# Four phases of a conditioned transformer in one program per engine, with the first sequences of a phase placed in the last iterations of the phase before it

## The reference

```python
# layer 0
h = film(rmsnorm(x, norm1_w), cond, film1_w, film1_b)        # x*(1+scale)+shift, per sequence
Q, K, V = h @ q_w + q_b, h @ k_w + k_b, h @ v_w + v_b
attn = softmax(einsum('bnd,bmd->bnm', Q, K) * D ** (-0.5))   # one head
x = x + (einsum('bnm,bmd->bnd', attn, V) @ proj_w + proj_b)
h = film(rmsnorm(x, norm2_w), cond, film2_w, film2_b)
x = x + gelu(h @ mlp_w1 + mlp_b1) @ mlp_w2 + mlp_b2          # 256 -> 1024 -> 256, erf gelu
# layer 1: cmod = silu(cond) @ w_ada + b_ada gives shift, scale and gate twice
k, q, v = split(modulate(layernorm(x), shift_msa, scale_msa) @ w_qkv)   # 16 heads of 16
w = softmax(einsum('bqhc,bkhc->bhqk', q / CH, k))
x = x + gate_msa * (einsum('bhqk,bkhc->bqhc', w, v) @ w_proj + b_proj)
h = gelu(modulate(layernorm(x), shift_mlp, scale_mlp) @ w_mlp1 + b_mlp1) # tanh gelu
x = x + gate_mlp * (h @ w_mlp2 + b_mlp2)
```

## Time and profile before

| | |
|---|---|
| median of 3 runs | 1713.98 us (1713.98 to 1715.13) |
| the profiled execution | 1714.05 us |
| its span in the profile | 1712.1 us |
| PE busy | 1623.0 us, 95% of the span |
| DVE, ACT, POOL busy | 1279.9, 867.3, 477.7 us |
| mean granted clock of PE | 0.98 of full speed |

### The profile page before, as it was taken

The page is one execution under the profiler, slowest core; times in us unless marked ns, Lnnn a source line. Parts: engine busy times, 40 slices in busy tenths (PEclk is TensorE's granted clock), DMA queues, the critical chain, the costliest instruction groups (busy, mean ns, idle before and its releaser), DMA issues. The chain is left out here.

```text
span 1712.1 us, 42938 instructions
## 1 busy us (share of the span) xinstructions
PE 1623.0 (95%) x14686; PEld 1455.3 (85%) x14686; DVE 1279.9 (75%) x2831; ACT 867.3 (51%) x1756; POOL 477.7 (28%) x633
## 2 busy tenths in 40 slices
PE   7999998999999997799999999999995999999998
PEld 6999997999999997577777777777763999999998
DVE  3798886676666664688888888888883777777776
ACT  1576663333333333577777777777764333333332
POOL 1333231122121212134333333433323121222211
PEclk8999999999999998899999999999997999999999
DMA  6500001000000000433333333333330111111111
GB/s 201 161 22 19 21 16 52 3 3 1 0 0 0 0 0 7 127 101 107 103 99 102 106 103 98 103 100 98 102 92 20 38 48 40 48 38 49 37 49 37
DMA packets 99465, 100.60 MB, mean 59 GB/s; under 512 B 13745, under 2 KB 89841, under 8 KB 99393
## 3 DMA queue, kind: packets, MB, share of 16 engines
q1 hardware_dynamic: 96784, 99.53, 18.5%
q10 hardware_dynamic: 2448, 0.08, 0.1%
q0 software_dynamic: 160, 0.04, 0.1%
HBM read 38.62 MB, written 8.55 MB: 28 GB/s over the span
## 5 line engine op out<-in xcount | busy, mean ns | idle before, releaser
L1403 DVE TENSOR_REDUCE C_negmax<-bank 128x4 f32<-128x1024 f32 x256 | 313.3, 1224 | 77.9 <-PE bank L1233 74.5
L1339 ACT ACTIVATE C_probs<-bank 128x1024 f32<-128x1024 f32 x256 | 262.1, 1024 | 116.6 <-PE bank L1247 113.8
L897 ACT ACTIVATE B_g<-bank,B_bias 128x256 f32<-128x256 f32 x256 | 107.3, 470 | 226.4 <-PE bank L198 208.6
L897 ACT ACTIVATE D_g<-bank,D_bias 128x256 f32<-128x256 f32 x256 | 107.3, 470 | 218.9 <-PE bank L198 218.9
L1233 PEld LDWEIGHTS bank<-C_kx,C_qs 64*128 64x128 f32 x1024 | 77.8, 187 | 114.6 <-DVE C_negmax L1403 78.4
L1233 PE MATMUL bank<-C_kx,C_qs 64*128 64x256 f32 x1024 | 130.5, 333 | 29.1 <-DVE C_negmax L1403 12.4
L198 PE MATMUL bank<-B_wt_w_hi,B_g_lo 128*128 128x256 f32 x512 | 147.6, 288 | 4.3 <-DVE B_g_lo L926 4.1
L198 PE MATMUL bank<-D_h_hi,D_wt_w_lo 128*128 128x256 f32 x512 | 147.6, 288 | 1.8 <-DVE D_h_lo L323 1.8
L198 PE MATMUL bank<-D_wt_w_hi,D_g_lo 128*128 128x256 f32 x512 | 146.9, 287 | 2.5 <-DVE D_g_lo L926 1.9
L198 PE MATMUL bank<-B_h_hi,B_wt_w_lo 128*128 128x256 f32 x512 | 147.2, 288 | 1.8 <-DVE B_h_lo L323 1.8
L198 PE MATMUL bank<-B_h_hi,B_wt_w_hi 128*128 128x256 f32 x512 | 145.5, 284 | 0.0
(11 more groups left out here) (263 smaller groups left out, 5090.0 us busy)
## 6 DMA issues: line engine op xcount, KB each, us to landing
C_qs<-C_q_hi SPq DMA_DIRECT2D x128, 128.0 KB
C_kx<-C_k_hi SPq DMA_DIRECT2D x128, 128.0 KB, 2.1
C_qs<-C_q_lo SPq DMA_DIRECT2D x64, 128.0 KB
C_kx<-C_k_lo SPq DMA_DIRECT2D x64, 128.0 KB, 2.1
C_gbc<-mod_rows SPq DMA_DIRECT2D x32, 256.0 KB, 3.4
D_gbc<-mod_rows SPq DMA_DIRECT2D x32, 256.0 KB, 3.3
out<-xres SPq DMA_DIRECT2D x32, 256.0 KB, 3.5
xres<-in_x SPq DMA_DIRECT2D x4, 1792.0 KB, 16.3
```

The costliest lines, as they stand in the source:

```text
L897: ins = eng.activation(g[u][:, d * S:(d + 1) * S], hbank[u][:, d * S:(d + 1) * S], func, bias=per_seq(bias1, 2 * u + d, b))
L1339: e_exp.by(eng.activation(probs[t % NP][:, :], stpair[:, :], ACT.Exp, scale=scl))
L1403: e_max.by(eng.tensor_reduce(m4[:, :, :, j], spair[:, :].rearrange("p (e q k) -> p e q k", e=2, q=TH), AX, ALU.max, negate=True))
```

## The change

One block holds the program of each engine for all four phases, one behind the other; the barriers between the phases are gone (the prologue keeps its block). Steps for the first sequences of a phase ("heads") are called from the last iterations of the phase in front:

- in A: stats, root, xhat, transposes and both splits of B's sequence 0. B then begins at iteration 1 (`START`).
- in B, iterations 28 to 32 (`TAIL` leaves four more iterations of B written out, so that they can differ): the first fill of C's stacks, stats, root, xhat, transposes and splits of C's sequences 0 and 1, q and k of sequence 0 with their splits, and on SP, behind the preparation's loads, the placing of q and k of sequence 0 (`head_place`, 14 transfers). C begins at iteration 1, without the tasks in `TAKEN`.
- in C: stats, root, xhat, transposes, splits of D's sequences 0 and 1, all four up products, gelus and splits of sequence 0 and three of its four down products; load and splits of D's `w2` in four parts; the first two loads of D's gates. D begins at iteration 2.

So that this can be, the norm has two sets of buffers (A and C, B and D), B and D use other banks, the tiles lie in other places, and where tiles of two phases share memory a wait stands in the program: `e_res.wait(..., LAST)`, the last residual of the phase in front, on ACT before B's first gelu, on POOL, on SP before the first loads, and at the start of C's ACT, POOL and SP programs. The once-only loads of C's and D's gate rows are made from `gates` directly. The core of the diff, without the lines that only change their indentation:

```diff
-def run_pipeline(eng, n_seq, max_skew, iteration):
+def run_pipeline(eng, n_seq, max_skew, iteration, first=0, tail=0):
-    for i in range(PEEL):
+    for i in range(first, PEEL):
         iteration(Seq(None, i))
-    with eng.Fori(PEEL // UNROLL, n_seq // UNROLL) as j:
+    with eng.Fori(PEEL // UNROLL, (n_seq - tail) // UNROLL) as j:
...
-    for i in range(n_seq, n_seq + max_skew):
+    for i in range(n_seq - tail, n_seq + max_skew):
...
+        attention_norm, mlp_norm = NormBuffers("a_"), NormBuffers("m_")
...
# phase A
+                NEXT_PE = {"B T": 541}
+                NEXT_ACT = {"B hi": 546}
+                NEXT_DVE = {"B stats": 523, "B xhat": 536.5, "B lo": 547}
+                NEXT_POOL = {"B root": 527}
...
# phases B and D
+                if l1:
+                    hbank, tbank = banks[:4], banks[4]
+                else:
+                    hbank, tbank = [banks[i] for i in (0, 1, 3, 4)], banks[2]
+                obank, head_bank = [banks[7], banks[5]], banks[7]
+                START, TAIL = (2, 0) if l1 else (1, 4)
...
                 def tensor(eng):
                     def it(i):
                         f, m, r = i, i.back(1), i.back(2)
+                        last = i.off if not l1 and i.reg is None else None
                         up(eng, m, 0)
                         down(eng, r, 3)
                         up(eng, m, 1)
                         down(eng, m, 0)
+                        if last == NB - 1:
+                            heads["C"].head_k(eng)
                         up(eng, m, 2)
                         down(eng, m, 1)
                         if f.exists(NB):
                             norm.e_lo.wait(eng, f.back(1))
                             norm.transpose(eng, f)
+                        if last in (NB - 2, NB):
+                            heads["C"].head_T(eng, last - NB >= 0)
                         up(eng, m, 3)
...
                         down(eng, m, 2)
+                        if last == NB - 2:
+                            heads["C"].head_q(eng)
...
                 def scalar(eng):
+                        if last == 1:
+                            prev.e_res.wait(eng, LAST)
+                        if last == NB - 1:
+                            heads["C"].head_hi(eng, "q")
                         for u in range(3):
                             gelu(eng, m, u)
+                        if last in (NB - 4, NB - 3):
+                            heads["C"].head_stacks(eng, last - NB + 4)
+                        if last == NB - 1:
+                            heads["C"].head_hi(eng, "k")
                         if f.exists(NB):
                             norm.evac_hi(eng, f)
+                        if last in (NB - 2, NB):
+                            heads["C"].head_hi(eng, "h", last - NB >= 0)
...
+                    def sync(eng):
+                        prev.e_res.wait(eng, LAST)
+                        prep.sync(eng)
+                        heads["C"].head_place(eng)
...
# phase C
+                NEXT_PE = {"D T": 525.95, "D up0": 538, "D up1": 540, "D T1": 541, "D up2": 547.6, "D up3": 548,
+                           "D down0": 549.5, "D down1": 550.5, "D down2": 555}
+                NEXT_ACT = {"D hi": 525.98, "D w2 hi0": 535.1, "D w2 hi1": 536.1, "D w2 hi2": 537.1, "D w2 hi3": 540,
+                            "D hi1": 540.3, "D gelu0": 542.1, "D gelu1": 542.2, "D gelu2": 544.6, "D gelu3": 546}
+                NEXT_DVE = {"D stats": 516, "D xhat": 521, "D lo": 535, "D stats1": 535.01, "D xhat1": 538.7, "D lo1": 543.99,
+                            "D split0": 552, "D split1": 553, "D split2": 560.1, "D split3": 560.2}
+                NEXT_POOL = {"D root": 517, "D w2 lo0": 543.4, "D w2 lo1": 543.5, "D root1": 535, "D w2 lo2": 543.8,
+                             "D w2 lo3": 543.9, "D xb": 560}
+                NEXT_SP = {"D w2": 532, "D gates": 553, "D gates1": 554}
+                TAKEN = [(n, 0) for n in ("lo_q", "lo_k", "z0", "z1", "q0", "q1", "k0", "k1")] + [
+                    (n, 1) for n in ("stats", "root", "xhat", "T", "hi_h", "lo_h")]
...
+                        if b.reg is None and (name, b.off) == ("q", 1):
+                            prev.e_res.wait(eng, Seq(None, NB - 2))
+                        if b.reg is None and (name, b.off) == ("M0", 0):
+                            prev.e_res.wait(eng, LAST)
+                    def d_T(b):
+                        e_vev.wait(eng, LAST)
+                        heads["D"].norm.transpose(eng, FIRST, heads["D"].head_bank)
+                    def d_up(b, u):
+                        (e_max if u < 2 else e_exp).wait(eng, LAST, NT)
+                        heads["D"].up(eng, FIRST, u)
...
+                    prev.e_res.wait(eng, LAST)
+                    eng.wait_ge(s_pad, 1)
+                    init_stacks(eng, 1)
...
+        with nc.Block() as blk:
+            @blk.tensor
+            def _(eng):
+                for n in "ABCD":
+                    heads[n].tensor(eng)
...
```

More of the change, by code:

```diff
@@ new lines, in down @@
+                def down(eng, b, u):
+                    if not b.exists(NB):
+                        return
+                    if l1 and b.reg is None and b.off == 0:
+                        eng.wait_ge(w2.s_lo, u + 1)
+                        if u == 0:
+                            norm.e_lo.wait(eng, SECOND)
+                    e_glo.wait(eng, b, u + 1)
+                    if u == 0:
+                        e_res.wait(eng, b.back(UNROLL))
+                    for h in range(TH):
+                        for d in range(2):
+                            c = slice(d * S + h * P, d * S + (h + 1) * P)
+                            ins = mm3(eng, obank[b.par][:, h * D:(h + 1) * D],
+                                      [((g_hi[u][:, c], g_lo[u][:, c]), w2.part(2 * u + d, 0, D))],
+                                      start=u == 0 and h == 0 and d == 0, stop=u == 3 and d == 1, skip=True)
+                    e_mm2.by(ins)
@@ new lines, in qk_cm @@
+                def qk_cm(eng, b, name, bank=None):
+                    bank = mbank(name) if bank is None else bank
+                    norm.e_lo.wait(eng, b)
+                    w_hi, w_lo = w_qk[name]
+                    for t in range(KT):
+                        c = [slice(k * D + t * P, k * D + (t + 1) * P) for k in range(KT)]
+                        ins = mm3(eng, bank[:, t * S:(t + 1) * S],
+                                  [((w_hi[:, c[k]], w_lo[:, c[k]]), norm.tokens(b, k)) for k in range(KT)])
+                    done[name].by(ins)
@@ new lines, in hi_bias @@
+                def hi_bias(eng, b, name, bank=None):
+                    bank = mbank(name) if bank is None else bank
+                    landed, dmas = (s_qd, Q_DMAS) if name == "q" else (s_kd, K_DMAS)
+                    prev_b = b.back(1)
+                    if not prev_b.before_first():
+                        for w in range(2):
+                            eng.wait_ge(landed[w][prev_b.par], (prev_b.pair + 1) * dmas * 16)
+                    done[name].wait(eng, b)
+                    for t in range(KT):
+                        c = slice(t * S, (t + 1) * S)
+                        ins = eng.activation(qk[name + "_hi"][:, c], bank[:, c], ACT.Identity, bias=per_seq(prep.bias[name], t, b))
+                    done_hi[name].by(ins)
```

1469 lines of the change are left out of this document (796 added, 673 removed).

## The result

The changed kernel takes 1672.82 us (median; executions from 1669.01 to 1675.84), the kernel before, run beside it, 1714.51 us: a ratio of 0.9756, 95% interval 0.973 to 0.9781. The forecast was 1670.0 in 1660 to 1686.

The account below looks back on a forecast made before the run. PE, busy 95% of the span, was taken to set the pace, with time to gain only where it idles or runs slowly. 7.5 + 17.5 + 19 = 44 us off 1714 gave 1670 us, range 1660 to 1686.

Parts of the forecast that it names:

- A to B: Change from phase A to B: first down product 7.5 us earlier, near 266.1; bounds 5 and 8.5 us.
- The rule of the added drain: Table switches at B's gelu and in D: the skill's drain would cost 1.4 us more each, 2.8 in all.
- B to C: Change from phase B to C: 17.5 us earlier, 16 of it at C's first score product; bounds 12 and 19.
- The 1.5 us for the clock: C's start: q product of sequence 1 at the upper clock gives back 12 x (0.245 - 0.119) = 1.5 us.
- C to D: Change from phase C to D: D's steady part 19 us earlier; bounds 14.7 and 23.5 us.
- hold the exponential chain by ...: C's tail: up groups and AV's product hold exponentials 2.9 us, w2 pieces 0.9, evacuation 0.2; last ends near 1301.9, not 1297.9.
- Within a steady iteration nothing changes: Steady loops: only bank numbers and buffer places change, costed at nothing, since PE at 99% and 97% covers them.
- The signs named: Profile after: B's first down product near 266, C's first score near 664.5, its eighth 15 to 17 us later.
- The drains only stretch: Rival, all three seams: drains lengthen, only barrier, norm and placing are saved, 24.6 us, giving 1689 us; chance 0.21.
- The barrier stays in another form: Rival, phase changes: waits for the last residual keep heads from running earlier, time within 0.2%, 1713 us; chance 0.02.
- The thin stretches stay cold: Rival, C's first two iterations and D's head: low clock costs 5 us, 1675 us; included in the 0.74 case.
- a head step stop PE for 3 us: Slower rival, last iterations: the change loses once 14 inserted PE steps wait 3.1 us each on average; chance 0.03.

Follow-up runs that it names:

- the first profile: Profiled execution of the changed kernel as it stands, beside the trace of the kernel before: 1675.45 us, span 1673.5 us.
- the second profile: The changed kernel, unaltered, profiled again beside the later experiments; its median there was 1671.92 us.

## Why the prediction was right, and where it was not

The total was met within 3 us, partly by luck: two seams gave 6 to 8 us less than forecast, and B's loop gave 5.7 that no step had.

*A to B: 7.5 taken, about 6 us at the higher clock and 4.6 in the first profile, below the bound of 5.* These are the ledger's 7.08 and 5.66 less the 1.1 us by which A's last three residuals lie further apart than before (17.83 us, 16.74 before); in two other traces with A unchanged they are 17.4 and 17.7 us apart, so with only the 0.4 of the wait taken off it is 6.7 and 5.3. The longer wait at A's end (0.4) and the table load (1.28, no more) came as walked. Residual to first down product shrank by 6.98, so 6.6 net: of the missing 0.9, half is the subtraction at 1.10 us beside POOL's addition, for which I took the 0.69 that a lone one needs, the rest ACT's start 0.5 us behind the residual. The difference of the two profiles is the clock. In the first profile it fell behind PE's wait of 2.48 us (0.68 granted in the 5 us behind it), in the second it did not behind 2.47 us (1.00), and the ledger's row differs by 1.4 us accordingly. The rule of the added drain, weighed in the prediction at 2.8 us for both switches, has no trace in any run: from the end of the exponential to the start of the gelu it is 1.32 us, load included.

*B to C: 17.5 taken, 17 measured.* The ledger gives 19.43 + 0.68 less 3.1 for the products that moved into B; undoing the head gives 17 to 18, of which 2.5 are that run's own. The walk held in its parts: the transposes, q and k fit B's iterations, the last iteration waits 0.71 us, the transfers went out on SP from 641.87 on, the second pair of fills costs DVE 0.27 us of waiting for q. The 1.5 us for the clock did not come as told: the q product of sequence 1 ran at the upper level, but the clock fell at 669.8, and the end of k and all of v ran at 0.21 us each. That is also the price of a matmul at the lower level: the prediction's 0.245 is a group's length through twelve, and the rows of before start 0.21 us apart, so twelve give back 1.1 us and not 1.5.

*C to D: 19 taken, 14.4 measured, below the bound of 14.7.* The step that failed is "hold the exponential chain by ..., so the last exponential ends near 1301.9 instead of 1297.9", 4.0 us; the stretch grew by 8.7 to 9.2. Inside the last sequence it was walked well: from its first to its last exponential 12.59 us before and 16.21 after. The other 5.0 us lie in front of it. I had left out DVE: "D lo" and the stats of sequence 1 stand in its order in front of two maxima, and the first of them waits for ACT's split; the last sequence's first exponential follows the one before it by 4.70 us instead of 1.85, and by 1.86 with these steps moved back. The remaining 2.15 us are in the exponentials of the sequence before (17.09 us instead of 14.94, and 17.08 with the steps moved): in one place D's xhat, 1.15 us on DVE, stands in front of a maximum, in the other D's first transposes and their split on ACT stand between two exponentials (3.94 us apart instead of 2.63). I had costed the queue of ACT and of PE in the last sequence and not DVE's, though the walk of each moved step past each queue was the method. Behind the last exponential the forecast fits: 12.0 us to the end of the projection against 12.1.

*"Within a steady iteration nothing changes ... there is nothing else to lose to": wrong.* B's loop was not at its limit; collisions hid below the resolution of PE's busy time. That the collision costs this is shown, by the waits added before and after. Why B escaped it in part after the change is not settled. The banks are excluded. Part of it is the race that 0.04 us decide, but a pair of residuals with both subtractions long takes 24.0 us after and 24.4 before, so even where the race is lost the collision costs less. Which of the moved buffers, instructions or starting moments does this is open.

*The signs named.* B's first down product stood at 270.62 us instead of 266, the 4.0 us of a later A included. C's first score product stood at 664.38 where 664.5 had been told, and that is luck: A's later end and the shortfall at A to B are hidden by B's faster loop. Its distance to the eighth, 16.1 us, and C's last projection behind D's up products came as told.

*The rivals.* "The drains only stretch" is refuted in its size: C's tail did stretch by 8.7 us, but the whole came out 41 us shorter. "The barrier stays in another form": putting real ones back cost 7 us. "The thin stretches stay cold" holds in part: in after the granted clock was 0.50 from 270.4 to 273.8, 669.8 to 676.6, 680.0 to 686.8 and 1263.7 to 1267.1 us. The first cost 1.4 us, which the second profile does not have; the price of the others is not isolated. Nowhere in B's or C's last iterations did a head step stop PE for 3 us; the longest was the 2.5 for the maximum.

## What to carry to other kernels

Cut two traces at the same events and book every difference before believing a total that came out as forecast: here it hid one gain and two shortfalls of nearly the same size. When work is moved in front of a drain, list what it passes on every engine's queue, and try its order there: the same DVE steps lay 2 us worse in front of the maxima and 5 us worse in front of their split than behind it (599.87, 603.32 and 598.22 us for the stretch). In a loop where PE looks 99% busy, look at the weight loads' column and at DVE and POOL operations on SBUF that start together: one wait that orders them was worth 8 to 12 us.

## What the runs showed of the hardware that was not expected

- A DVE subtraction of 128x512 and two POOL additions of 128x256 (1.42 us for both where nothing of DVE runs beside them): begun behind POOL, the subtraction took 1.10 to 1.29 us in 525 of 525 cases; begun up to 0.62 us ahead of it and beside no other POOL instruction, 0.69 us in 78 of 86. Where POOL was ahead by less than 0.4 us, its two additions took 1.87 to 2.08 us in all but two cases.
- The lower clock does not follow from the length of one gap: in front of B's first down product PE waited 2.48, 2.48, 2.48 and 2.04 us in four profiles in which the granted clock of the 5 us behind it was 0.66 to 0.71, and 2.48, 2.48, 2.47, 2.47 and 2.04 us in five others in which it stayed at 1.00.
- It does not need a gap that the profile shows either: in three profiles (325.5, 327.9 and 332.5 us) it fell to 0.50 for 3.4 us in the middle of B while PE was busy for the whole of it and for 9.94 of the 10 us in front, in the second of them. Each time it cost about 1.6 us. The eleven other profiles do not have it.
- A switch from Exp to Gelu costs its load of 1.28 us and 0.04 around it.
